# Turning q and k of three attentions by DMA transposes from SP, with expert weights issued from ScalarE

## The chip, the cores and the metric

The program runs on one core of one Trainium2 chip. The metric is the device time of one execution in microseconds (us), from launch to the last instruction on the slowest core; here there is only one core. Lower is better.

## The reference

Six layers are applied in turn to x (16 batch elements of 256 tokens x 256 channels, float32), with a layer norm of the residual sum after each:

```python
x = _layernorm(x + _L0_attn_ref(x, ...))                # a: 16 heads of 16, rotary, Taylor softmax
x = _layernorm(x + _L0_xattn_ref(x, ctx, ctx, mask))    # b: 16 heads, masked softmax, keys from ctx
x = _layernorm(x + _L0_ffn_ref(x, ...))                 # c: 8 experts, two chosen per token
x = _layernorm(x + _L1_attn_ref(x, ...))                # d: convolutions, delta rule, two FIR filters
x = _layernorm(x + _L1_xattn_ref(x, ctx, ctx))          # e: 16 heads, softmax, no projections
x = _layernorm(x + _L1_ffn_ref(x, ...))                 # f: FP4-rounded gate/up/down
```

In b and e:

```python
scores = jnp.einsum('bhqd,bhkd->bhqk', Q, K) / math.sqrt(D_K)
attn = jax.nn.softmax(scores, axis=-1)
context = jnp.einsum('bhqk,bhkd->bhqd', attn, V)
```

Layer a has (1 + s + s*s/2), divided by its sum, in place of the softmax. Layer d convolves each channel causally with 4 taps (q, k, v), and v again with 3 and with 31 taps.

## The kernel before

**Stages and lags.** Each batch element passes through the layers a, b, c, d, e, f. Iteration n of the program works on element n in a and b, n-1 in c, n-2 in d, n-3 in e and f (`LAG`, line 65), so 19 iterations are made and 13 of them hold all six layers. Within an iteration the order of the work is written out by hand: `BODY` (line 96) is one list of named segments, and every engine runs its own part of each segment in that order. Each engine executes in order, so an instruction that waits holds back everything that stands behind it on its engine.

**q and k of an attention.** q and k are split into bf16 parts that together keep float32 precision: for each token and head, six terms of 16 columns are laid side by side in `split` (96 columns, 102 with the columns for the mask and the row maximum). ScalarE makes casts and copies (`part_copies`, L1205), VectorE the differences (`split_rest`, L1550 and L1556); the last write of VectorE raises the signal p3, the last of ScalarE `copies`. A score product needs heads on partitions by their columns, so `split` must be turned: TensorE does this (`split_turn`, L731), 32 transposes for q and 32 for k in each attention, through the PSUM banks 0 to 3 (`turn_qk`). ScalarE (L1215) and VectorE (L1564) each copy two of the four banks of q and of k into `qT` and `kT`. In b and e the products `maxima` (L752) follow, whose row maxima VectorE takes (L1571); then three columns of `split` are filled with the shift and q is turned again (`turn_again`, segment `again`), and the final scores are made (L765).

**What stands around the turns in an iteration.** For e: `d_in c_in e_turnq e_turnk c_gate e_max0 d_proj e_max1`. For b: `b_turnq b_turnk d_scan2 b_max0 d_scan3`. For a: `a_turnq c_up2a c_up2b c_down2a f_round0 d_fir0 d_place c_down2b a_turnk c_up3a c_up3b c_down3a f_round1 d_fir1 c_down3b c_up4a c_up4b`, and the first score only later, after `f_down` and `d_one4`. The segments `f_round0` and `f_round1` are VectorE's FP4 rounding (from L1448 to L1457), whose result TensorE transposes (L1149).

**SP's queue.** SP issues all DMAs: inputs, the output, the small block DMAs of d (L544 to L559), and the expert weights (`layer_c`, L536 for c_w1, L538 for c_w2, 512 KB each). Two slots hold expert weights, so a load waits until TensorE has finished with the expert two before.

**VectorE's filters.** The taps of the convolution (L1749) and of the FIR filters (`fir`, L1788 and L1790) add into an accumulator. After each tap over all its channels comes `link`: the last instruction raises a semaphore and VectorE waits for it before the next tap.

```python
 def link(g, ins):
     chain[g] += 1
     ins.then_inc(s_chain[g], 1)
     dve.wait_ge(s_chain[g], chain[g])
```

Of the kernel before, what the change touches and what calls it, by code (L numbers as in the profile page):

```python
# [33 lines left out]
MASK0, MAX0, SLOT = QK, QK + 3, QK + 6  # L34
VS = 32
# [15 lines left out]
PT_SLOTS = 8  # L51
W_SLOTS = 2
CONSTANTS_MASK = 7
CONSTANTS = 54 - 4 * (LEVELS - 2) + 2
# [125 lines left out]
def bank_uses():  # L180
# [21 lines left out]
    turned("e", "turnq", "qT")  # L202
    turned("e", "turnk", "kT")
# [6 lines left out]
    for t in range(T):  # L210
        turned("a", "turn" + "qk"[t], "qk"[t] + "T")
        at(f"f_round{t}", (f"f_hT{t}a", 0), (f"f_hT{t}b", 1))
# [7 lines left out]
    turned("b", "turnq", "qT")  # L220
    turned("b", "turnk", "kT")
# [36 lines left out]
def decoder(nc, d, out):  # L258
    ctx = ExitStack()
    with ctx:  # L260
# [62 lines left out]
        yf, yc, yd = tok("yf"), tok("yc"), tok("yd")  # L323
# [51 lines left out]
        eye = sb("eye", [P // 2, BB, BB])[:, :, :]  # L375
# [12 lines left out]
        fshort, flong, qn, kn, kb, vb, vt, uu, dd = (sub(2, S) for _ in range(9))  # L388
        beta = sb("beta", [P, T, DH])
# [15 lines left out]
        f_sc = sb("f_sc", [P, 2, FF // BLK])  # L405
# [17 lines left out]
        for l in "abe":  # L423
            att[l] = {n: signal(f"{l}_{n}", 1) for n in
                      ("p1", "r1", "p2", "p3", "copies") + (("src",) if l != "e" else ("v",)) + (("shift",) if l != "a" else ())}
        c_diff = signal("c_diff", 1)
# [62 lines left out]
        def _(sp):  # L489
# [32 lines left out]

            def layer_a(b):
# [4 lines left out]
                sp.dma_start(ctxf[:, :, :], at(d["ctx"], b)).then_inc(*ctxf_in.up)  # L528

            def layer_c(b):  # L530
                for e in range(E):
                    yield "c_in" if e < W_SLOTS else f"c_up{e - 1}a"
                    slot = e % W_SLOTS
                    before = (e - W_SLOTS, b) if e >= W_SLOTS else (E + e - W_SLOTS, b - 1)
                    sp.wait_ge(*PS.filled(f"c_h{before[0]}_1", before[1]))
                    sp.dma_start(c_w1[:, slot], d["c_w1"][e].rearrange("(c p) n -> p c n", p=P)).then_inc(*c_w1in[slot].up)  # L536
                    sp.wait_ge(*PS.filled(f"c_y{before[0]}", before[1]))
                    sp.dma_start(c_w2[:, slot], d["c_w2"][e].rearrange("(c p) n -> p c n", p=P)).then_inc(*c_w2in[slot].up)  # L538
# [22 lines left out]
            def layer_e(b):  # L561
                yield "e_in"
                sp.wait_ge(*xo["x6_ready"](b, 0))
                sp.dma_start(ctxb[:, :, :], at(d["ctx"], b)).then_inc(*ctxb_in.up)

# [5 lines left out]
            batches(sp, {"a": layer_a, "c": layer_c, "d": layer_d, "e": layer_e, "f": layer_f})  # L571
# [4 lines left out]
        def _(pool):  # L576
# [38 lines left out]
            for l in range(BASE, LEVELS - 1):  # L615
# [10 lines left out]
            made(pool.memset(eye, 0.0))  # L626
            made(pool.affine_select(out=eye, in_=eye, compare_op=ALU.not_equal, fill=1.0, base=0,
                                    pattern=[[1, BB], [-1, BB]], channel_multiplier=0))
# [32 lines left out]
            def layer_d(b):  # L661
# [8 lines left out]
                step(pool.tensor_copy(blkT, eye))  # L670
# [23 lines left out]
        def _(pe):  # L694
# [1295 lines left out]
```

## Time and profile before

| | |
|---|---|
| median of 3 runs | 4020.27 us (4013.6 to 4021.18) |
| the profiled execution's own time | 4020.32 us |
| its span, first to last instruction | 4018.6 us |
| TensorE matmul / weight load busy | 83% / 63% |
| VectorE, ScalarE, GpSimd busy | 65%, 41%, 8% |
| mean granted TensorE clock | 0.932 of full |
| DMA engines busy, mean | 14.2% of 16 engines by the main queue, 171.27 MB |

The profile is one execution. A row of the timeline gives the start in us from the span's start, the duration in us, the engine, the line, the operation, output and input with their shapes, the count of merged instructions, and in brackets the idle time before it with what ended that. PE is TensorE's matmuls (transposes among them), PEld its weight loads, DVE VectorE, ACT ScalarE, POOL GpSimd, SPq SyncE's DMA issues. The granted clock (PEclk) is 1.00 at 2.4 GHz and 0.50 at 1.2 GHz.

### The profile page before, as it was taken

Reading aid. Unit: us, or ns where it says so; the run is one execution under the profiler, and the core shown is the slowest. Engines: PE = TensorE matmul, PEld = TensorE weight load, DVE = VectorE, ACT = ScalarE, POOL = GpSimd, SP = SyncE. Lnnn points to the kernel's source line nnn. Section 1 sums busy time; section 2 is a strip of 40 time slices with the busy share of each in tenths; the row PEclk is TensorE's granted clock in tenths of the full one; section 3 lists DMA queues with packets and bytes.
Section 4 is the critical chain, followed back from the end, with each engine's and each line's share of the span. In section 5 each row is a group of like instructions: output and inputs, shape, how many; then the busy total and the mean of one; then the engine's idle time right before and its main releaser. Section 6 shows DMA issues by size and latency. Waiting matters only on the chain.

```text
span 4018.6 us, 58753 instructions
## 1 busy us (share of the span) xinstructions
PE 3319.1 (83%) x22532; PEld 2516.8 (63%) x22532; DVE 2621.5 (65%) x5927; ACT 1637.0 (41%) x3066; POOL 341.3 (8%) x696
## 2 busy tenths in 40 slices
PE   1678988889898988889898888989898888978664
PEld 0356766767676676767576676767576676756442
DVE  4324667685776767676676768577676768666653
ACT  1433453444435354443435354443535344442311
POOL 1000101010100101010100101010010101010100
PEclk9788999999999999999999999999999999999776
DMA  2011202111111112111111111111111211111000
GB/s 71 22 58 48 64 28 63 35 56 43 40 49 42 55 35 59 40 51 43 38 56 38 54 35 57 42 46 48 43 48 35 64 35 56 43 34 49 9 6 3
DMA packets 185713, 175.03 MB, mean 44 GB/s; under 512 B 59208, under 2 KB 147936, under 8 KB 185440
## 3 DMA queue, kind: packets, MB, share of 16 engines
q1 hardware_dynamic: 185440, 171.27, 14.2%
q8 instruction: 186, 3.05, 0.3%
q14 instruction: 87, 0.71, 0.1%
HBM read 156.55 MB, written 14.68 MB: 43 GB/s over the span
## 4 chain that ended last, share of the span: by engine, by line
PE 51%; DVE 28%; ACT 10%; issue 6%; POOL 3%; DMA 1%; PEld 0%; SPq 0%; PEldq 0%; DVEq 0%; POOLq 0%; ACTq 0%
PE bank L697 18%; PE bank L932 6%; ACT pt_f L1194 5%; DVE nm_f L1571 5%; PE bank L731 5%; PE bank L785 4%; DVE region L1790 4%; PE bank L765 3%; ACT qT_f L1215 2%; PE bank L1014 2%; PE bank L778 1%; PE bank L752 1%; PE bank L1093 1%; PE bank L1025 1%; POOL rn L666 1%
## 5 line engine op out<-in xcount | busy, mean ns | idle before, releaser
L1194 ACT ACTIVATE pt_f<-bank 128x512 f32<-128x512 f32 x768 | 416.2, 594 | 281.8 <-PE bank L765 280.1
L932 PE MATMUL bank<-c_w,c_hb 128*128 128x256 f32 x2048 | 509.4, 388 | 9.8 <-PEq L1167 6.4
L697 PE MATMUL bank<-xTc,c_w 128*128 128x256 f32 x2048 | 485.6, 386 | 15.6 <-DVE yc L1723 14.5
L1790 DVE SCALAR_TENSOR_TENSOR region<-vpad,cols,region 128x256 f32<-128x256 f32 x1024 | 450.5, 481 | 15.4
L932 PEld LDWEIGHTS bank<-c_w,c_hb 128*128 128x128 f32 x2048 | 377.4, 192 | 97.1 <-issue 25.8
L697 PEld LDWEIGHTS bank<-xTc,c_w 128*128 128x128 f32 x2048 | 381.4, 192 | 77.7 <-DVE yc L1723 20.2
L1293 ACT ACTIVATE c_hb<-bank,cols 128x256 f32<-128x256 f32 x512 | 215.0, 471 | 476.6 <-PE bank L697 476.6
L1571 DVE TENSOR_REDUCE nm_f<-bank 128x2 f32<-128x512 f32 x512 | 315.6, 683 | 127.6 <-PE bank L752 125.5
L731 PE MATMUL bank<-identb,split_f 128*102 128x128 bf16 (+1 forms) x4096 | 291.8, 239 | 113.8 <-DVE split_f L1556 72.7
L765 PE MATMUL bank<-qT_f,kT_f 102*128 102x256 bf16 (+1 forms) x1536 | 276.8, 282 | 115.7 <-ACT pt_f L1194 92.7
L731 PEld LDWEIGHTS bank<-identb,split_f 128*102 128x102 bf16 (+1 forms) x4096 | 279.3, 142 | 144.3 <-DVE split_f L1556 86.0
L765 PEld LDWEIGHTS bank<-qT_f,kT_f 102*128 102x128 bf16 (+1 forms) x1536 | 112.5, 98 | 278.7 <-ACT pt_f L1194 221.6
L1215 ACT COPY qT_f<-bank 102x1024 bf16<-102x1024 bf16 (+1 forms) x160 | 156.1, 1014 | 166.0 <-PE bank L731 166.0
L1194 ACT ACTIVATE xTf<-bank 128x512 f32<-128x512 f32 x112 | 66.8, 597 | 353.6 <-PE bank L706 324.8
L785 PE MATMUL bank<-pt_f,v_f 128*32 128x256 f32 x3072 | 205.8, 394 | 0.4 <-PEq L1167 0.3
L1723 DVE SCALAR_TENSOR_TENSOR yc<-bank,comb,yc 128x256 f32<-128x256 f32 x256 | 111.8, 478 | 134.6 <-PE bank L932 127.3
L643 POOL TENSOR_TENSOR rstd_f<-ve_f,neghalf 128x2 f32<-128x2 f32 x80 | 57.1, 714 | 1608.2 <-DVE ve_f L1533 1608.2
L1564 DVE COPY qT_f<-bank 102x1024 bf16<-102x1024 bf16 (+1 forms) x160 | 110.5, 691 | 117.2 <-PE bank L731 117.2
L1827 DVE TENSOR_TENSOR region<-region,bank 128x512 f32<-128x512 f32 x128 | 85.1, 685 | 119.1 <-PE bank L1025 110.0
L1205 ACT COPY split_f<-split_f 128x512 bf16<-128x512 bf16 x288 | 159.6, 618 | 3.0
L697 PE MATMUL bank<-f_wgu,xTf 128*128 128x352 f32 x512 | 157.9, 467 | 0.7 <-ACT xTf L1194 0.7
L752 PE MATMUL bank<-kT_f,qT_f 99*128 99x256 bf16 x1024 | 145.6, 280 | 10.3 <-DVE kT_f L1564 3.9
(310 smaller groups left out, 5470.8 us busy)
## 6 DMA issues: line engine op xcount, KB each, us to landing
c_w<-in_c_w SPq DMA_DIRECT2D x256, 512.0 KB, 3.9
gram_scratch<-region SPq DMA_DIRECT2D x32, 256.0 KB, 2.2
x<-in_x SPq DMA_DIRECT2D x16, 256.0 KB, 4.4
x<-in_ctx SPq DMA_DIRECT2D x16, 256.0 KB, 4.5
ctxb<-in_ctx SPq DMA_DIRECT2D x16, 256.0 KB, 4.3
out_dram<-x SPq DMA_DIRECT2D x16, 256.0 KB, 2.2
region<-gram_scratch SPq DMA_DIRECT2D x128, 8.0 KB
inverse_scratch<-region SPq DMA_DIRECT2D x32, 64.0 KB
```

What stands on the lines that cost most here:

```text
L697: mm = pe.matmul(out_ap, l, r, start=(i == 0), stop=(i == len(pairs) - 1))
L731: mm = pe.transpose(o[0:n, j, t * P:(t + 1) * P], a.split[:, t, which, 4 * i + j, 0:n], identb[:, :])
L752: mm = pe.matmul(PS[use][:, t * S:(t + 1) * S], a.qT[0:MAX0, h, t * P:(t + 1) * P], a.kT[0:MAX0, h, :], start=True, stop=True)
L765: mm = pe.matmul(PS[use][:, c * S:(c + 1) * S], a.kT[0:rows_, h, c * P:(c + 1) * P], a.qT[0:rows_, h, :], start=True, stop=True)
L785: mm = pe.matmul(o[32 * j:32 * j + 32, :], a.v[:, c, h, :], a.pt[:, h % PT_SLOTS, c, :], start=(c == 0 and not taylor), stop=(c == T - 1), ...
L932: mm = pe.matmul(PS[use][:, t * D:(t + 1) * D], c_hb[:, k, t * P:(t + 1) * P], c_w2[:, e % W_SLOTS, k, :], start=(k == 0), stop=(k == HC - 1))
L1194: act.activation(dst, PS[use].rearrange("p (c s) -> p c s", c=c), func, **kw).then_inc(*PS.drained(use))
L1205: ins = act.copy(slot(n), slot(0) if n else per_head(src[:, :, :]))
L1215: act.copy(dst[0:n, 4 * i:4 * i + 4, :], PS[f"{use}{i}"].bitcast(BF16).rearrange("p (h s) -> p h s", h=4)[0:n])\
L1293: ins = act.activation(c_hb[:, k, :], PS[use][:, i * S:(i + 1) * S], ACT.Relu, bias=col("b1")[:, e * HC + k:e * HC + k + 1])
L1571: dve.tensor_reduce(a.nm[:, :, h], PS[use].rearrange("p (t s) -> p t s", t=T), AX.X, ALU.max, negate=True)\
L1790: ins = dve.scalar_tensor_tensor(dst[:, c, :], x, w_[:, c, k:k + 1], dst[:, c, :], ALU.mult, ALU.add)
```

## The change

1. **Turning by DMA.** `split` is padded from 102 to 128 columns a head, and `qT`, `kT` to 128 partitions. `turn_qk` and its copies on ScalarE and VectorE are gone from a, b and e. SP waits for p3, `copies` and the last earlier score, and then issues eight DMA transposes for each attention, each of [128 tokens, 8 heads x 128 columns] in bf16 (256 KB): four for heads 0 to 7 (signal `turned0`), four for heads 8 to 15 (`turned1`). TensorE waits for `turned0` ahead of the first group of heads and for `turned1` ahead of the third. The second turn of q in b and e (`again`) stays on TensorE.
2. **Expert weights from ScalarE.** The loads c_w1 and c_w2 leave SP and are issued by ScalarE: experts 0 and 1 at the start of `c_in`, expert e+1 behind the activations of `c_up{e}a`.
3. **VectorE's waits.** The convolution, the FIR filters and the layer norm's statistics wait for the tap (or half) that they add to, no longer for all of the tap before (`mark` in the place of `link`).
4. **Room.** `yd` shares memory with `fshort`, `f_sc` lies in `pt`; the block identity `eye` is no longer kept: GpSimd makes it in place each time (a memset and a select instead of a copy).

```diff
-                s.split = sb(f"split_{g}", [P, T, 2, H, SLOT], BF16)
-                s.qT = sb(f"qT_{g}", [SLOT, H, S], BF16)
-                s.kT = sb(f"kT_{g}", [SLOT, H, S], BF16)
+                s.split = sb(f"split_{g}", [P, T, 2, H, PITCH], BF16)
+                s.qT = sb(f"qT_{g}", [P, H, S], BF16)
+                s.kT = sb(f"kT_{g}", [P, H, S], BF16)
...
+            def turn_heads(b, l, last, half):
+
+                if half == 0:
+                    sp.wait_ge(*att[l]["p3"](b))
+                    sp.wait_ge(*att[l]["copies"](b))
+                    sp.wait_ge(*PS.filled(*last))
+                n = H // HALVES
+                for i, dst in enumerate((at_.qT, at_.kT)):
+                    for t in range(T):
+                        sp.dma_start_transpose(dst[:, half * n:(half + 1) * n, t * P:(t + 1) * P],
+                                               at_.split[:, t, i, half * n:(half + 1) * n, :].rearrange("p h d -> p (h d)")
+                                               ).then_inc(*att[l][f"turned{half}"].up)
+
+            def turns(b, l, last):
+                yield f"{l}_turnq"
+                turn_heads(b, l, last, 0)
+                yield f"{l}_turnk"
+                turn_heads(b, l, last, 1)
...
-            def turn_qk(b, l, a, n):
-                yield f"{l}_turnq"
-                pe.wait_ge(*att[l]["p3"](b))
-                pe.wait_ge(*att[l]["copies"](b))
-                for i in range(4):
-                    split_turn(b, l, a, n, f"{l}_qT", 0, i)
-                yield f"{l}_turnk"
-                for i in range(4):
-                    split_turn(b, l, a, n, f"{l}_kT", 1, i)
-
             def maxima(b, l, a, g):
-                if g == 0:
-                    for i in range(4):
-                        pe.wait_ge(*PS.taken(f"{l}_kT{i}", b))
+                if g % 2 == 0:
+                    pe.wait_ge(*att[l][f"turned{g // 2}"](b))
...
+            def load_expert(b, e):
+
+                slot = e % W_SLOTS
+                before = (e - W_SLOTS, b) if e >= W_SLOTS else (E + e - W_SLOTS, b - 1)
+                act.wait_ge(*PS.filled(f"c_h{before[0]}_1", before[1]))
+                act.dma_start(c_w1[:, slot], d["c_w1"][e].rearrange("(c p) n -> p c n", p=P)).then_inc(*c_w1in[slot].up)
+                act.wait_ge(*PS.filled(f"c_y{before[0]}", before[1]))
+                act.dma_start(c_w2[:, slot], d["c_w2"][e].rearrange("(c p) n -> p c n", p=P)).then_inc(*c_w2in[slot].up)
+
             def layer_c(b):
                 yield "c_in"
+                for e in range(W_SLOTS):
+                    load_expert(b, e)
                 evac(b, "c_xT", xTc[:, :, :])
...
                         ins.then_inc(*PS.drained(use))
+                        if m == 0 and W_SLOTS <= e + 1 < E:
+                            load_expert(b, e + 1)
...
+            def mark(g, ins):
+
+                chain[g] += 1
+                ins.then_inc(s_chain[g], 1)
+                return chain[g]
...
                         if k == 0:
                             ins = dve.tensor_scalar(dst[:, c, :], x, w_[:, c, 0:1], None, ALU.mult)
                         else:
+                            dve.wait_ge(s_chain["d"], summed[c])
                             ins = dve.scalar_tensor_tensor(dst[:, c, :], x, w_[:, c, k:k + 1], dst[:, c, :], ALU.mult, ALU.add)
-                    return ins
+                        if (K, k, c) == (KL, KL - 1, C - 1):
+                            ins.then_inc(*d_fir.up)
+                        else:
+                            summed[c] = mark("d", ins)
```

**How it moves instructions: SP.** On SP before, from the inputs of a to just behind the blocks of d (in_c_w is an expert's weights, gram_scratch and inverse_scratch hold the blocks of d):

```order
L526 DMA x<-in_x 128x2x256
L528 DMA x<-in_ctx 128x2x256
L544 DMA gram_scratch<-region 128x512 x2
L549 DMA region<-gram_scratch 8x16x16 x8
L536 DMA c_w<-in_c_w 128x2x512
L538 DMA c_w<-in_c_w 128x4x256
L553 DMA inverse_scratch<-region 8x8x256 x2
L559 DMA region<-inverse_scratch 16x16x16 x8
L536 DMA c_w<-in_c_w 128x2x512
L538 DMA c_w<-in_c_w 128x4x256
```

The same stretch now:

```order
L544 DMA x<-in_x 128x2x256
L546 DMA x<-in_ctx 128x2x256
L556 DMA gram_scratch<-region 128x512 x2
L561 DMA region<-gram_scratch 8x16x16 x8
L531 DMA_TRANSPOSE qT_f<-split_f 128x8x128 x2
L531 DMA_TRANSPOSE kT_f<-split_f 128x8x128 x2
L565 DMA inverse_scratch<-region 8x8x256 x2
L571 DMA region<-inverse_scratch 16x16x16 x8
L531 DMA_TRANSPOSE qT_f<-split_f 128x8x128 x2
L531 DMA_TRANSPOSE kT_f<-split_f 128x8x128 x2
```

The sixteen weight loads of an iteration left the queue and 24 transposes came in; the first four of a stand ahead of the block DMAs of `d_place`.

**TensorE, around the turns of b.** Before, from the last `c_up6a` to the first maxima (L731 turns, L1060 to L1073 are `d_scan2`, L752 maxima):

```order
L697 MATMUL bank<-xTc,c_w 128x256 x4
L731 MATMUL bank<-identb,split_f 102x128 x64
L1060 MATMUL bank<-region 128x64 x2
L1062 MATMUL bank<-Sb,wTn 128x64 x2
L1060 MATMUL bank<-region 128x64 x2
L1062 MATMUL bank<-Sb,wTn 128x64 x2
L1073 MATMUL bank<-region 128x64 x4
L752 MATMUL bank<-kT_f,qT_f 128x256 x8
```

Now:

```order
L709 MATMUL bank<-xTc,c_w 128x256 x4
L1058 MATMUL bank<-region 128x64 x2
L1060 MATMUL bank<-Sb,wTn 128x64 x2
L1058 MATMUL bank<-region 128x64 x2
L1060 MATMUL bank<-Sb,wTn 128x64 x2
L1071 MATMUL bank<-region 128x64 x4
L753 MATMUL bank<-kT_f,qT_f 128x256 x8
```

The 64 transposes are gone; only `d_scan2` stands between p3 and the maxima, which now wait for `turned0`.

**ScalarE, at the start of c.** Now, from the last split copies of e to the gate (xTd and xTc are the transposed inputs of d and c):

```order
L1202 COPY split_f<-split_f 128x2x16x16 x2
L1191 ACTIVATE xTd<-bank 128x512
L1271 DMA c_w<-in_c_w 128x2x512
L1273 DMA c_w<-in_c_w 128x4x256
L1271 DMA c_w<-in_c_w 128x2x512
L1273 DMA c_w<-in_c_w 128x4x256
L1191 ACTIVATE xTc<-bank 128x512
L1282 ACTIVATE gw<-gw 128x2
```

The four loads of experts 0 and 1 stand between xTd and xTc, just behind p3 of e; before they stood on SP, and the turn copies of e stood here behind xTc.

## Rows read from the trace of the kernel before

**Rows 1.** The page, parts 1 and 4: busy time by engine, and the chain.

```profile
PE 3319.1 (83%) x22532; PEld 2516.8 (63%) x22532; DVE 2621.5 (65%) x5927; ACT 1637.0 (41%) x3066; POOL 341.3 (8%) x696
...
PE 51%; DVE 28%; ACT 10%; issue 6%; POOL 3%; DMA 1%; PEld 0%; SPq 0%; PEldq 0%; DVEq 0%; POOLq 0%; ACTq 0%
```

**Rows 2.** Timeline around the turns of e, iteration 7; d_w is d_proj.

```profile
1477.10 1.29 DVE L1556 TENSOR_TENSOR split_f<-rest_f,split_f 128x512 bf16<-128x512 f32 x2 [1.21 <-ACT split_f L1205]
1478.45 5.96 PE L731 MATMUL bank<-identb,split_f 128*102 128x128 bf16 x64 [3.12 <-DVE split_f L1556]
1478.63 0.59 ACT L1194 ACTIVATE xTc<-bank 128x512 f32<-128x512 f32 x1
...
1484.24 1.01 PE L697 MATMUL bank<-c_wg,xTc 128*128 128x8 f32 x8
...
1485.39 1.03 PE L752 MATMUL bank<-kT_f,qT_f 99*128 99x256 bf16 x8
```

**Rows 3.** Windows of 1 us there: busy us by engine, PEclk, DMA share, GB/s.

```profile
1476.00:1477.00 1.00, 0.00 (x0) 0.00 (x0) 0.00 (x0) 1.00 (x2) 0.00 (x0) 0.62 0.00 0
...
1483.00:1484.00 1.00, 1.00 (x20) 1.00 (x19) 0.45 (x1) 1.00 (x2) 0.00 (x0) 0.96 0.00 0
```

**Rows 4.** Timeline around the turns of b, same iteration.

```profile
1645.97 1.29 DVE L1556 TENSOR_TENSOR split_f<-rest_f,split_f 128x512 bf16<-128x512 f32 x2 [1.82 <-ACT split_f L1205]
...
1647.47 4.01 PE L731 MATMUL bank<-identb,split_f 128*102 128x128 bf16 x64
...
1651.31 0.61 PE L1060 MATMUL bank<-region 128*128 128x64 f32 x4
...
1654.54 1.04 PE L752 MATMUL bank<-kT_f,qT_f 99*128 99x256 bf16 x8
```

**Rows 5.** Windows elsewhere in that iteration: an idle TensorE, and the clock.

```profile
1533.00:1534.00 1.00, 0.00 (x0) 0.00 (x0) 1.00 (x1) 0.21 (x1) 0.29 (x1) 1.00 0.40 147
1534.00:1535.00 1.00, 0.00 (x0) 0.00 (x0) 1.00 (x4) 0.00 (x0) 0.00 (x0) 0.64 0.92 342
```

**Rows 6.** Timeline around the turns of a: L1448 starts a rounding, L1149 uses it.

```profile
1556.49 1.99 PE L731 MATMUL bank<-identb,split_f 128*96 128x128 bf16 x32
...
1559.12 0.87 DVE L1448 TENSOR_REDUCE f_sc<-pt_f 128x44 f32<-128x704 f32 x1
...
1565.78 0.87 PE L1149 MATMUL bank<-ident,pt_f 128*128 128x128 f32 x6 [1.73 <-DVE pt_f L1457]
...
1577.33 4.54 DVE L1790 SCALAR_TENSOR_TENSOR region<-vpad,cols,region 128x256 f32<-128x256 f32 x10
1577.47 0.88 PE L1149 MATMUL bank<-ident,pt_f 128*128 128x128 f32 x6 [1.73 <-DVE pt_f L1457]
...
1582.84 1.99 PE L697 MATMUL bank<-xTc,c_w 128*128 128x256 f32 x8 [1.04 <-DVE yc L1723]
```

**Rows 7.** VectorE's convolution in the timeline, six independent taps between waits.

```profile
1504.96 7.41 DVE L1749 SCALAR_TENSOR_TENSOR region<-region,cols 128x256 f32<-128x256 f32 x18
```

**Rows 8.** The page, part 6: DMA issues, KB each, median us to landing.

```profile
c_w<-in_c_w SPq DMA_DIRECT2D x256, 512.0 KB, 3.9
gram_scratch<-region SPq DMA_DIRECT2D x32, 256.0 KB, 2.2
```

**Rows 9.** Windows with DMA at work: pieces of 64 bytes, then weights.

```profile
1563.00:1564.00 1.00, 1.00 (x4) 0.59 (x4) 0.97 (x2) 0.00 (x0) 0.00 (x0) 1.00 0.35 33
...
1567.00:1568.00 1.00, 1.00 (x6) 0.87 (x5) 0.96 (x3) 0.26 (x2) 0.00 (x0) 1.00 0.87 332
```

**Rows 10.** Timeline of SP's issues: a weight load, the blocks, and one iteration later.

```profile
1500.54 0.37 SPq L536 DMA_DIRECT2D c_w<-in_c_w  x1
...
1561.37 3.77 SPq L559 DMA_DIRECT2D region<-inverse_scratch  x8
...
1645.77 0.51 SPq L564 DMA_DIRECT2D ctxb<-in_ctx  x1
...
1729.24 0.37 SPq L536 DMA_DIRECT2D c_w<-in_c_w  x1
```

More of the change, by code:

```diff
@@ L528, in layer_a, with layer_b @@
                 sp.dma_start(ctxf[:, :, :], at(d["ctx"], b)).then_inc(*ctxf_in.up)
[L530 to L538, printed above, removed]
+                yield from turns(b, "a", ("e_s15", b - LAG["e"]))
+            def layer_b(b):
+                yield from turns(b, "b", ("a_s15", b))
             def layer_d(b):
@@ L564, in layer_e @@
                 sp.dma_start(ctxb[:, :, :], at(d["ctx"], b)).then_inc(*ctxb_in.up)
+                yield from turns(b, "e", ("b_s15", b + LAG["e"] - 1))
             def layer_f(b):
@@ L669, in layer_d @@
                 step = lambda ins: link(ins)
-                step(pool.tensor_copy(blkT, eye))
+                step(pool.memset(blkT, 0.0))
+                step(pool.affine_select(out=blkT, in_=blkT, compare_op=ALU.not_equal, fill=1.0, base=0,
+                                        pattern=[[1, BB], [-1, BB]], channel_multiplier=0))
                 pool.wait_ge(*d_blocks_in(b))
@@ L854, in layer_a @@
                 to_tokens(b, "a_v", xTf, a_wv)
-                yield from turn_qk(b, "a", a, QK)
                 for g in range(4):
                     yield f"a_score{g}"
-                    if g == 0:
-                        for i in range(4):
-                            pe.wait_ge(*PS.taken(f"a_kT{i}", b))
+                    if g % 2 == 0:
+                        pe.wait_ge(*att["a"][f"turned{g // 2}"](b))
                     yield from heads(b, "a", a, g, QK, True)
@@ L883, in layer_b @@
                 to_tokens(b, "b_q", xTf, b_w[:, 0])
-                yield from turn_qk(b, "b", a, SLOT)
                 for g in range(4):
@@ L1113, in layer_e @@
             def layer_e(b):
-                yield from turn_qk(b, "e", a, SLOT)
                 for g in range(4):
@@ L1241, in layer_a @@
                 part_copies(b, "a", a, qs, ks, 2)
-                yield "a_turnq"
-                turned(b, a, "a_qT", a.qT, QK)
-                yield "a_turnk"
-                turned(b, a, "a_kT", a.kT, QK)
                 for g in range(4):
@@ L1526, in ln_stats @@
             def ln_stats(b, l, g, src):
+                made = [mark(g, dve.bn_stats(stats[g][:, t, :], src[:, t, :])) for t in range(T)]
                 for t in range(T):
-                    ins = dve.bn_stats(stats[g][:, t, :], src[:, t, :])
-                link(g, ins)
-                for t in range(T):
+                    dve.wait_ge(s_chain[g], made[t])
                     ins = dve.bn_aggr(mv[g][:, t, :], stats[g][:, t, :])
@@ L1748, in layer_d @@
                             dve.wait_ge(*PS.taken(f"d_{'qkv'[j // 2]}", b))
+                        if k:
+                            dve.wait_ge(s_chain["d"], tapped[j])
                         ins = dve.scalar_tensor_tensor(cv[:, j, :], pre[:, j, k:k + S], w[:, j, k:k + 1], cv[:, j, :], ALU.mult, ALU.add)
-                    link("d", ins) if k < 2 else ins.then_inc(*d_cv.up)
+                        if k < 2:
+                            tapped[j] = mark("d", ins)
+                ins.then_inc(*d_cv.up)
                 yield "d_silu"
@@ L1796, in filters @@
                     for k in range(i * len(taps) // n, (i + 1) * len(taps) // n):
-                        ins = fir(*taps[k])
-                        if k == len(taps) - 1:
-                            ins.then_inc(*d_fir.up)
-                        else:
-                            link("d", ins)
+                        fir(*taps[k])
                 yield "d_fir0"
```

44 lines of the change are left out of this document (11 added, 33 removed).

## The prediction

> **What bounds the kernel now.** I read the page's busy times and chain first: TensorE is busy 83% and carries 51% of the chain, VectorE 28%, ScalarE 10% [rows 1]. No engine bounds alone; the bound changes from place to place, so a saving counts where its engine is waited for. The issue rows of the trace give the length of a full iteration: the same weight load comes at 1500.54 and 1729.24 [rows 10], so 228.7 us, and what is worked out for one iteration counts 16 times (each attention is run 16 times; the partial iterations at both ends are taken as alike). Then I read the timeline at the three places where q and k are turned, and the windows for the clock.
>
> - At e [rows 2] everything waits in a line: p3 ends at 1478.39, TensorE has stood for 3.12 us, makes 64 transposes in 5.96 us and starts the maxima at 1485.39, **7.0 us after p3**. The windows say why 64 transposes take 5.96 here and 4.01 at b [rows 2, 4]: the granted clock is at 0.62 in the slice from 1476 and 0.96 in the slice from 1483 [rows 3]; between them TensorE ran at 1.2 GHz.
> - At b [rows 4] p3 ends at 1647.26, the transposes take 4.01 us, `d_scan2` from 1651.31 on, and the maxima start at 1654.54, **7.3 us after p3**, 3.2 of which are `d_scan2`.
> - At a [rows 6] the first score comes over 30 us after p3, so a transfer is hidden there. VectorE's rounding is the bound: TensorE waits 1.73 us for each of the two.
>
> **The change, part by part.**
>
> *The wait for a transfer, L.* L is the time from p3 until four DMA transposes (1 MB) have landed. No transpose by DMA is in this trace, so a transfer of 256 KB is bounded from both sides. Plain pieces of 1 to 2 KB: the window with weights moves 332 GB/s at a share of 0.87 [rows 9], 382 at a full share, so 0.68 us. Pieces of 64 bytes: 33 GB/s at 0.35 [rows 9], 94 at a full share, so 2.8 us (at the 33 really moved, 8 us). A turned transfer is likely cut into more pieces than a plain one but into none below 64 bytes; I take 1.1 us, nearer to the plain end because a head's row is 256 bytes. The latency comes on top: 256 KB leave SBUF in 2.2 us [rows 8], 1.5 without the transfer. Alone, L = 1.5 + 4 x 1.1 = 5.9 us; the ends are 4.2 and 12.7.
> The page "DMA: Bandwidth & Descriptors", section "Latency and other measured facts", of the Trainium skill gives DMA transposes 261 GB/s. By that, 1.0 us for each and L = 5.5, an estimate; no run here shows it so far.
>
> *Weights in the way.* ScalarE now issues the four loads of experts 0 and 1 between the copies of xTd and xTc, just behind p3 of e, at 1478.7 in the old times; at 0.37 us an issue [rows 10] all four are out 1.5 us later. They are 2 MB, 5.4 us of the DMA engines at 382 GB/s, beside the first transposes. At b the two loads of expert 7 come 1.2 us after p3: 2.7 us. Before, they were issued earlier, beside nothing urgent. If the two queues share the engines evenly, half of that lies in front: L is 5.9 + 2.7 = **8.6 at e** and 5.9 + 1.3 = **7.2 at b**. The bounds are none and all.
>
> *e.* TensorE loses 64 transposes but cannot start the maxima before p3 + 8.6: 8.6 - 7.0 = +1.6 us. And the low clock, which the transposes used to bear, now falls on other work. It rose 4.6 us after steady work began (1478.45 to about 1483.0 [rows 2, 3]); those 4.6 us now begin with the maxima and `d_proj`, which do half as much in them: +2.3. Together **+3.9 us**. ScalarE's 1.5 us of issues in front of xTc only delay the gate, which ends in the wait.
>
> *b.* TensorE reaches the maxima at p3 + 3.3 and waits till 7.2: 7.2 - 7.3 = -0.1. It stands 3.9 us. After 2.5 us of standing the clock fell in the slice from 1534 [rows 5], so it falls here too: +2.3, none if the wait is short. **+2.2 us**. With the 4 us of transposes gone, what is late next is the transfer.
>
> *a.* Both transpose sets of 1.99 us go, and VectorE's four copies in front of the two roundings. The first rounding starts at the end of the yc addition, about 1557.4, in place of 1559.12 [rows 6], 1.7 us sooner; the second gains another 1.1 us from the copies and 0.3 from the filters between. So the second L1149 comes 3.1 us earlier, less than the 4.0 that TensorE gives up, because it waits for VectorE. Then ten FIR taps and the yc addition stand before the matmul at 1582.84: another 0.5. **-3.6 us**.
>
> *The links.* Ten FIR taps take 4.54 us, 0.454 each; the convolution, with a link every six, 0.412 [rows 6, 7]. Without waiting for the pair before, 0.1 us goes with each of 34 pairs: 3.4 us of VectorE an iteration. Where TensorE leads that is hidden; beyond the 0.8 counted at a I put **-0.5**.
>
> *ScalarE.* It loses 12 turn copies of 1 us an iteration and takes 16 issues of 0.37 us, always behind the activation that is waited for. At nothing; with that cover gone, at most 0.8 us at each of six places.
>
> *SP and the rest.* The blocks of `d_place` stood at 1561.37 [rows 10]; four transposes of a now precede them, 4.4 us, and TensorE asks for them 20 us later, so nothing. The context for e, issued at 1645.77, waits for eight transposes of b until about 1656 and is read at 1697: nothing. The weights for `c_up3a` are no longer behind the block DMAs. GpSimd's two instructions for one stand in its wait for the blocks. PSUM banks come free earlier. All at nothing.
>
> *Sum.* 3.9 + 2.2 - 3.6 - 0.5 = +2.0 us an iteration, times 16 = +32 us on the profiled execution's own 4020.32 (0.05 us above the median): **4052 us**, 0.8% slower. The sign turns on L: with the clock's price at both places the sum is zero where the two L have a mean of 6.9 us; the forecast has 7.9.
>
> **The rivals.**
>
> 1. *The transfer is short, and the kernel faster.* Place: the same two waits. If a transpose moves like a plain transfer, 0.68 us, and the queues hardly disturb each other, L is 4.2. At e, the gate (held by ScalarE's issues) holds the maxima until about p3 + 4.6: -2.4 +2.3. At b p3 + 4.2: -3.1, and the 0.9 us of standing leaves the clock alone. With -4.1: -7.3 an iteration, -117 us, 3903 us. For it: the engines are busy only 14% on average. Against it: the loads behind p3, and that small pieces moved far slower than weights [rows 9]. It decides from L below 6.9.
> The page "Advanced Engine Details and Errata", section "X-Bar Transpose (TRN2)", of the Trainium skill says that transposing DMAs are as fast as plain ones on this chip; that is this rival, and no row here shows it yet. I give it 0.3.
> 2. *The transfer is long.* At 2.8 us a transpose L is 12.7 at both: e +5.7 +2.3, b +5.4 +2.3, with -4.1: +11.6, +186 us, 4206 us. For it: many small pieces, and a queue whose issuing may itself take the time. Against it: at 94 GB/s the pieces of 64 bytes were bound by their issue. 0.2.
> 3. *ScalarE's queue is late with the weights.* Expert 4's first load would be issued near 1570 and read near 1576.6; landing takes 3.9 [rows 8], a slack of 2.6 us that transposes of a might eat. If each of six loads came 1 us late: +6 - 4.1 + 6.1, about +8, +128 us, 4148. 0.05.
> 4. That the change does not do what it says would be a second wait in place of the transposes at a too; its scores come 30 us later, so I give it no chance of its own.
>
> **How the numbers follow.** Forecast 0.45, rival 1 0.3, rival 2 0.2, rival 3 0.05. The forecast's own range, from L between 6.2 and 9.5 without or with the clock at b, is 3990 to 4100. The whole range takes in the values of rivals 1 and 2: 3900 to 4210. Faster by over 0.2% (8 us, about what a measurement of this kernel can tell from no change): 0.3 and 0.07 of the forecast, 0.37. Within 0.2%: 0.08. Slower: 0.55.
>
> **What would show it.** In the changed profile: the gap from p3 to the maxima at e (8.6 here, 7.0 before) and at b (7.2, 7.3 before); a TensorE that waits for DMA there; the granted clock still at 0.5 in `d_proj` and falling after p3 of b; `c_up4b` 3.6 us closer to p3 of a; filter taps of 0.41 us. An L under 6 at both places, or a clock that stays up, would make the forecast wrong, and so would a VectorE or ScalarE relief that shortens stretches between these three places, which I have put at 0.5 us.

## The result, and the profile after

The kernel as changed takes 4166.69 us (median of 4 runs, 4159.63 to 4177.01) where the one before, on the same chip, takes 4016.93: a ratio of **1.0368** (95% interval 1.0348 to 1.0388), 150 us or 9.4 us an iteration slower. 4052 was forecast: the sign was right, the loss almost five times too small. The profiled execution took 4171.6 us, its span 4169.9, the mean granted clock 0.878 (0.932 before).

The page, parts 1, 4 and 6, of the changed kernel, for [rows 1] and [rows 8]:

```profile
PE 3207.2 (77%) x19460; PEld 2399.0 (58%) x19460; DVE 2447.8 (59%) x5735; ACT 1451.0 (35%) x2874; POOL 348.3 (8%) x710
...
PE 47%; DVE 24%; ACT 10%; SPq 7%; issue 6%; DMA 3%; POOL 2%; PEldq 0%; DVEq 0%; POOLq 0%; ACTq 0%; PEld 0%
...
c_w<-in_c_w ACTq DMA_DIRECT2D x256, 512.0 KB, 4.8
...
qT_f<-split_f SPq DMA_TRANSPOSE x192, 4.3
kT_f<-split_f SPq DMA_TRANSPOSE x192, 3.4
```

TensorE is busy for 112 us less than before, VectorE for 174, ScalarE for 186 (GpSimd for 7 more), and the kernel is slower: work was taken off the engines and a wait put in its place. The chain has 7% of SP's queue and 3% of DMA, which had 0 and 1. The view of waits, of TensorE (engine, line, whose end it waited for, us in total, times, longest), names it:

```profile
PE bank L753 <- DMA kT_f<-split_f: 281.3, 35, 16.7
```

**Around e** (timeline, for [rows 2]; `d_w` is d_proj):

```profile
1521.63 1.29 DVE L1559 TENSOR_TENSOR split_f<-rest_f,split_f 128x512 bf16<-128x512 f32 x2 [1.20 <-ACT split_f L1202]
...
1521.65 0.37 ACTq L1271 DMA_DIRECT2D c_w<-in_c_w  x1
...
1522.96 5.74 SPq L531 DMA_TRANSPOSE qT_f<-split_f  x2
1528.74 4.01 SPq L531 DMA_TRANSPOSE kT_f<-split_f  x2
1532.80 2.71 SPq L531 DMA_TRANSPOSE qT_f<-split_f  x2
...
1534.86 1.89 PE L753 MATMUL bank<-kT_f,qT_f 99*128 99x256 bf16 x8 [8.67 <-DMA kT_f<-split_f]
1536.55 7.64 PE L709 MATMUL bank<-xTd,d_w 128*128 128x256 f32 x24
```

p3 ends at 1522.92. The two pairs of transposes of heads 0 to 7, with weights beside them, hold SP's queue for 5.74 and 4.01 us; the pair after them, nearly alone, for 2.71. The maxima start at 1534.86, **11.9 us after p3**, where it was 7.0. The windows there (columns as in [rows 3]):

```profile
1516.00:1519.00 3.00, 0.66 (x4) 0.42 (x4) 2.66 (x10) 1.61 (x4) 0.88 (x2) 1.00 0.00 0
...
1523.00:1526.00 3.00, 1.68 (x8) 1.69 (x8) 0.00 (x0) 0.86 (x2) 0.00 (x0) 0.50 0.96 318
...
1537.00:1541.00 4.00, 4.00 (x11) 3.19 (x10) 1.02 (x3) 0.80 (x2) 0.00 (x0) 0.50 1.17 150
1541.00:1545.00 4.00, 4.00 (x25) 3.55 (x24) 0.00 (x0) 2.64 (x7) 0.00 (x0) 0.98 0.33 111
```

TensorE idled and its clock went from 1.00 to 0.50; it is still at 0.50 (1.2 GHz) while d_proj runs without a gap from 1537 to 1541, and is back just behind. Before, with the clock up, the same products of `d_proj` took 5.35 us in place of 7.64, and the maxima 1.03 [rows 2] in place of 1.89:

```profile
1486.26 5.35 PE L697 MATMUL bank<-xTd,d_w 128*128 128x256 f32 x24
```

**Around b** (timeline, for [rows 4]), and two windows:

```profile
1693.28 1.29 DVE L1559 TENSOR_TENSOR split_f<-rest_f,split_f 128x512 bf16<-128x512 f32 x2 [1.82 <-ACT split_f L1202]
...
1694.60 2.81 SPq L531 DMA_TRANSPOSE qT_f<-split_f  x2
...
1694.99 0.42 ACTq L1271 DMA_DIRECT2D c_w<-in_c_w  x1
...
1697.45 6.66 SPq L531 DMA_TRANSPOSE kT_f<-split_f  x2
...
1706.10 1.89 PE L753 MATMUL bank<-kT_f,qT_f 99*128 99x256 bf16 x8 [7.97 <-DMA kT_f<-split_f]
```

```profile
1693.00:1696.00 3.00, 3.00 (x21) 2.56 (x20) 2.08 (x4) 2.38 (x6) 0.00 (x0) 1.00 0.07 13
...
1710.00:1715.00 5.00, 5.00 (x22) 4.07 (x23) 2.91 (x5) 1.68 (x4) 0.00 (x0) 0.50 0.37 89
```

p3 ends at 1694.57, so the maxima come **11.5 us after p3** (7.3 before). Here the first pair is through before the weights arrive and the second takes 6.66 us. The clock falls here too, where it stayed up before.

**All sixteen turns.** The two places above are one iteration. Counted from the timeline for every element (end of p3 to the first maxima), the median is **12.4 us at e** (7.0 before) and **10.3 us at b** (7.3 before): at e the place shown is on the low side, at b it is the longest of the sixteen. The last two turns of e, where the expert weights are no longer loaded, come 7.5 us after p3 in this same trace.

**Around a** (timeline, for [rows 6]), and the convolution and a piece of the FIR filters (for [rows 7]):

```profile
1608.68 1.28 DVE L1559 TENSOR_TENSOR split_f<-rest_f,split_f 128x512 bf16<-128x512 f32 x2
...
1632.27 1.99 PE L709 MATMUL bank<-xTc,c_w 128*128 128x256 f32 x8 [0.41 <-DVE yc L1718]
```

```profile
1559.04 7.16 DVE L1747 SCALAR_TENSOR_TENSOR region<-region,cols 128x256 f32<-128x256 f32 x18
...
1627.39 4.04 DVE L1794 SCALAR_TENSOR_TENSOR region<-vpad,cols,region 128x256 f32<-128x256 f32 x10
```

From p3 of a (1609.96; before, 1556.43) to `c_up4b` it is 22.3 us, where it was 26.4: 4.1 us gained, 3.6 forecast. A tap takes 0.40 us.

### The profile page after: what moved, and what is told of

Its sections match the earlier page's. It is cut to its first block, busy times and chain, and to the rows that moved or that the text cites. A ratio compares the mean times of both kernels' runs of the same rounds, so it can differ in the third digit from the quotient of the medians.

```text
span 4169.9 us, 52451 instructions
## 1 busy us (share of the span) xinstructions
PE 3207.2 (77%) x19460; PEld 2399.0 (58%) x19460; DVE 2447.8 (59%) x5735; ACT 1451.0 (35%) x2874; POOL 348.3 (8%) x710
## 4 chain that ended last, share of the span: by engine, by line
PE 47%; DVE 24%; ACT 10%; SPq 7%; issue 6%; DMA 3%; POOL 2%; PEldq 0%; DVEq 0%; POOLq 0%; ACTq 0%; PEld 0%
PE bank L709 16%; SPq L531 6%; ACT pt_f L1191 5%; PE bank L930 4%; PE bank L786 4%; PE bank L753 3%; PE bank L766 3%; DMA kT_f<-split_f 3%; ACT split_f L1202 2%; DVE nm_f L1574 2%; PE bank L1091 2%; DVE region L1794 2%; PE bank L1012 1%; PE bank L1023 1%; PE bank L779 1%
## 5 line engine op out<-in xcount | busy, mean ns | idle before, releaser
L709 PE MATMUL bank<-xTc,c_w 128*128 128x256 f32 x2048 | 500.6, 395 | 7.5 <-DVE yc L1718 6.7
L709 PEld LDWEIGHTS bank<-xTc,c_w 128*128 128x128 f32 x2048 | 396.5, 199 | 76.5 <-DVE yc L1718 12.7
L1794 DVE SCALAR_TENSOR_TENSOR region<-vpad,cols,region 128x256 f32<-128x256 f32 x1024 | 413.3, 477 | 0.0
L753 PE MATMUL bank<-kT_f,qT_f 99*128 99x256 bf16 x1024 | 190.3, 347 | 282.9 <-DMA kT_f<-split_f 281.3
L753 PEld LDWEIGHTS bank<-kT_f,qT_f 99*128 99x128 bf16 x1024 | 114.8, 120 | 338.8 <-DMA kT_f<-split_f 288.1
L709 PE MATMUL bank<-f_wgu,xTf 128*128 128x352 f32 x512 | 159.4, 471 | 12.6 <-DVE hf L1624 11.9
L1594 DVE RECIPROCAL rc_f<-bank 128x16 f32<-128x16 f32 x96 | 23.9, 249 | 204.9 <-PE bank L811 204.9
L709 PEld LDWEIGHTS bank<-f_wgu,xTf 128*128 128x128 f32 x512 | 98.3, 195 | 68.1 <-issue 17.6
L786 PEld LDWEIGHTS bank<-pt_f,v_f 128*32 128x32 f32 x3072 | 86.1, 111 | 84.5 <-issue 48.5
```

The lines of the kernel that those rows point to most:

```text
L709: mm = pe.matmul(out_ap, l, r, start=(i == 0), stop=(i == len(pairs) - 1))
L753: mm = pe.matmul(PS[use][:, t * S:(t + 1) * S], a.qT[0:MAX0, h, t * P:(t + 1) * P], a.kT[0:MAX0, h, :], start=True, stop=True)
L786: mm = pe.matmul(o[32 * j:32 * j + 32, :], a.v[:, c, h, :], a.pt[:, h % PT_SLOTS, c, :], start=(c == 0 and not taylor), stop=(c == T - 1), ...
L1794: ins = dve.scalar_tensor_tensor(dst[:, c, :], x, w_[:, c, k:k + 1], dst[:, c, :], ALU.mult, ALU.add)
```

## The experiments

Theory 1, after this reading: the loss is made at the two waits, at e and b, by the transfer, by the weight loads beside it and by the clock behind it; the rest of the change gains a little. Theory 2: ScalarE's queue, or DMA traffic in general, slows other work. Ratios are to the kernel before on the same chip, with their 95% intervals.

### One part at a time

**m_actw**: the kernel before, with part 2 (weights from ScalarE) alone.

```diff
-            def layer_c(b):
-                for e in range(E):
-                    yield "c_in" if e < W_SLOTS else f"c_up{e - 1}a"
...
+                        if m == 0 and W_SLOTS <= e + 1 < E:
+                            load_expert(b, e + 1)
```

> The kernel before with part 2 alone: the expert weights are issued from ScalarE at the places of the change, all turns stay on TensorE. Theory 1: without DMA transposes beside them the loads disturb nothing and ScalarE's issues lie behind what is waited for: within 0.2% of before (4010 to 4028). Theory 2 (ScalarE's queue is a cause of its own: its issues delay activations or come late with weights): 1 us or more at each of several experts, 4050 or more, and TensorE waiting for c_w in the waits.

Measured 4019.38 us, ratio 0.9991 (0.9982 to 1.0000). ScalarE's queue and the places of the loads cost nothing by themselves. Theory 2 has lost one half.

**m_marks**: the kernel before, with part 3 (VectorE's waits) alone.

```diff
+                            dve.wait_ge(s_chain["d"], summed[c])
                             ins = dve.scalar_tensor_tensor(dst[:, c, :], x, w_[:, c, k:k + 1], dst[:, c, :], ALU.mult, ALU.add)
...
-                            link("d", ins)
```

> The kernel before with part 3 of the change alone (VectorE waits for the tap it adds to, not for all of the tap before; the same in the layer norm's statistics). Theory 1 (the loss is made at the two waits for transfers, at e and b, and the other parts are small gains): FIR taps at 0.41 us in place of 0.454, 3 us of VectorE less in an iteration, of which 0.5 to 1.2 us count: 4000 to 4010 us, 0.2 to 0.5% faster than before. Rival (VectorE's taps are hidden everywhere, or the semaphores cost as much): within 0.1% of before.

Measured 4028.53 us, ratio 1.0018 (1.0006 to 1.0029): no gain. The expectation missed. VectorE's own work did become shorter (the FIR taps, before and here), and one of its waits for TensorE longer (before and here):

```profile
L1790 DVE SCALAR_TENSOR_TENSOR region<-vpad,cols,region 128x256 f32<-128x256 f32 x1024 | 450.5, 481 | 15.4
L1804 DVE SCALAR_TENSOR_TENSOR region<-vpad,cols,region 128x256 f32<-128x256 f32 x1024 | 413.2, 479 | 0.0
...
DVE yc L1723 <- PE bank L932: 127.3, 23, 16.3
DVE yc L1728 <- PE bank L932: 164.8, 37, 16.3
```

The 37 us that the taps save are waited away one step later, for TensorE. TensorE itself is busy for 19 us more than before [rows 1], at a mean granted clock of 0.921 for 0.932:

```profile
PE 3338.5 (83%) x22532; PEld 2533.1 (63%) x22532; DVE 2578.0 (64%) x5927; ACT 1635.2 (41%) x3066; POOL 339.3 (8%) x696
```

So its products were slower; why the clock is lower here is not known.

**m_aonly**: the change with e and b turned on TensorE as before; a alone is turned by DMA.

```diff
+PE_TURNS = "eb"
...
+                if l in PE_TURNS:
+                    if g == 0:
+                        for i in range(4):
+                            pe.wait_ge(*PS.taken(f"{l}_kT{i}", b))
```

> The changed kernel with the turns of e and b given back to TensorE; only those of a go through the DMA transposes. Theory 1: the 4.1 us that the changed kernel gains at a stay, and both losses go: 4.1 and 0.5 to 1 us of VectorE's waits, 16 times: 3935 to 3950 us, about 2% faster than before. Theory 2 (transposes or ScalarE's loads slow other work wherever they run): not faster than before, 4020 or more.

Measured **3949.86 us**, ratio **0.9831** (0.9810 to 0.9852), faster than both kernels; theory 2, which expected 4020 or more, has lost its other half. So what the change does at a, with the weights from ScalarE and the marks, is worth 68 us by the ratio (66 were forecast: 16 x 4.1), and turning e and b by DMA loses all of it and 150 us more, 13.6 us an iteration.

**m_alink**: the same without the marks (the diff of m_marks taken back).

> Only parts 1 and 2 of the change and a alone of part 1: e and b are turned on TensorE, VectorE keeps its links of before. It differs from the kernel with a alone (3949.86, a ratio of 0.9831) in the links. The links alone cost nothing when they were taken away by themselves (1.0018). Theory (a's transposes carry the whole gain, the marks none): 3940 to 3955, within 0.3% of that kernel. Rival (the marks do pay once a's VectorE stretch is what the end waits for): 3965 to 3985.

Measured 3975.71 us, ratio 0.9895 (0.9876 to 0.9913). The rival was right: the same marks that were worth nothing alone are worth 0.65% (26 us) once a is turned by DMA. The pages of m_alink and of m_aonly:

```profile
PE 3260.2 (82%) x21508; PEld 2465.3 (62%) x21508; DVE 2581.5 (65%) x5863; ACT 1576.4 (40%) x3002; POOL 348.5 (9%) x710
...
PE 3249.8 (82%) x21508; PEld 2456.6 (62%) x21508; DVE 2534.4 (64%) x5863; ACT 1574.8 (40%) x3002; POOL 347.4 (9%) x710
```

With the marks VectorE still waits 30 us longer for TensorE at the yc addition (159.9 us in m_aonly, 130.1 in m_alink), as it did in m_marks, so that wait does not decide. What differs is TensorE's busy time in the profiled executions: 19 us more by the marks alone, 10 us less here, which is of the size of the difference between a loss of 7 us and a gain of 26. Why its products become slower in the one case and not in the other was not tested.

### The loads beside the transposes

**m_noload**: the change, with the expert weights loaded only once.

```diff
             def load_expert(b, e):
-
+                if b or e >= W_SLOTS:
+                    return
```

> The changed kernel with all expert loads left out but the first two, so every expert uses the first weights (that part of the result is not computed); nothing shares the DMA engines with the transposes. Theory 1 in the form that the loads stretch the transposes: a pair takes 2.7 us everywhere, the wait from p3 to the maxima falls from 11.9 and 11.5 to about 7.4 us at e and b, and the time by 4.3 us at two places, 16 times, to about 4030. Rival (a transpose queue has such stalls by itself): the pairs of 4 to 6.6 us stay, 4150 or more.

Measured 4029.39 us, ratio 1.0022 (1.0011 to 1.0033): 137 of the 150 us go with the loads (123 by the shorter waits, 16 times 4.9 and 2.8 us; most of the rest is clock, since `d_proj` takes 105.7 us in all for 115.0 in the change). Timeline around e, and two windows inside b's and e's waits:

```profile
1464.59 2.60 SPq L531 DMA_TRANSPOSE qT_f<-split_f  x2
1467.24 2.71 SPq L531 DMA_TRANSPOSE kT_f<-split_f  x2
...
1472.01 1.89 PE L753 MATMUL bank<-kT_f,qT_f 99*128 99x256 bf16 x8 [4.69 <-DMA kT_f<-split_f]
```

```profile
1404.00:1407.00 3.00, 0.00 (x0) 0.00 (x0) 0.00 (x0) 0.00 (x0) 0.00 (x0) 0.50 1.05 195
...
1470.00:1472.00 2.00, 0.00 (x0) 0.00 (x0) 0.40 (x3) 0.00 (x0) 0.00 (x0) 0.50 1.04 195
```

Alone, a transpose of 256 KB takes 1.35 us, and the maxima come 7.4 us after p3 at this e. Over all sixteen turns the median is 7.5 us at e and 7.5 at b. Single pairs still take longer without weights (3.40 us at the b whose window is shown, which makes its wait 8.4 us); what disturbs them is not known. The windows say why loads hurt it so: **the transposes alone bring the share of the sixteen DMA engines to 1.04 at 195 GB/s**, where weights moved 332 at a share of 0.87 [rows 9]. So there was hardly a free share for a load to use, and what it takes, the transposes wait for.

**m_late**: the change whole, with the loads of experts 0, 1 and 7 issued by ScalarE once the transposes have landed.

```diff
+                for e in range(W_SLOTS):
+                    if b + LAG["c"] >= LAG["e"]:
+                        act.wait_ge(*att["e"][("turned0", "turned1")[e]](b + LAG["c"] - LAG["e"]))
+                    load_expert(b, e)
...
                 yield "d_scan3"
+                if b + 1 < NB:
+                    if b + 2 < NB:
+                        act.wait_ge(*att["b"]["turned1"](b + 2))
+                    load_expert(b + 1, E - 1)
```

> The change whole, with the same expert loads from ScalarE issued behind the transposes: expert 0 once heads 0 to 7 of e have landed, expert 1 and expert 7 once all sixteen have. Nothing is left out. Theory (the loads beside the transposes stretch the wait, the low clock follows): both waits shrink as in the kernel without loads, p3 to the maxima 9 us at most at e and 8 us at b, and the time is 4010 to 4050, where the change had 4167. Rival (the loads are in the way wherever they stand, or come too late for c_up0a and c_up7a now): above 4100, with TensorE waiting for c_w.

Measured 4182.01 us, ratio 1.0421 (1.0398 to 1.0444): neither. TensorE's wait fell as theory 1 has it (medians of 7.5 us after p3 at e and at b), but ScalarE got two new ones in its place (views of waits, TensorE and ScalarE):

```profile
PE bank L753 <- DMA kT_f<-split_f: 179.7, 35, 16.8
```

```profile
ACT region L1309 <- DMA kT_f<-split_f: 190.6, 14, 15.6
...
ACT region L1368 <- DMA kT_f<-split_f: 130.9, 13, 11.0
```

L1309 is ScalarE's first copy of d_proj, L1368 its first of `d_scan3`. L1309 stands behind the wait for all sixteen heads, and expert 0's load, issued after eight, stretched the second half (a pair of 7.57 us). The experiment had the flaw that the edit made a wait on an in-order engine with other work behind it.

**m_tail**: the same loads issued by SP instead, behind the transposes in its own queue.

```diff
+            def layer_c(b):
+                for e, name in ((0, "c_gate"), (1, "c_comb"), (E - 1, "c_up6b")):
+                    yield name
```

> The change whole, nothing left out, with the loads of experts 0, 1 and 7 back on SP, behind the eight transposes of e and of b in its queue; experts 2 to 6 stay on ScalarE. No instruction of ScalarE waits for a transpose, and no load stands beside one at e or b. Theory (m_late lost at ScalarE's two new waits what it won at TensorE's): the waits of TensorE for kT add up to about 180 us as in m_late, no wait of ScalarE for it, and the time is that of the kernel without loads, 4015 to 4045. Rival (behind the transposes the loads come too late for c_up0a and c_up7a): above 4080 with TensorE waiting for c_w.

Measured 4032.07 us, ratio 1.0037 (1.0024 to 1.0050), as expected, with nothing left out: 135 us of the 150 come back by the place of three loads an iteration. TensorE's wait:

```profile
PE bank L763 <- DMA kT_f<-split_f: 174.7, 35, 16.9
```

The maxima come 7.5 us after p3 at e and at b (medians), as in the kernel without loads.

### The size of a transpose

**m_quart**: the change with four groups of four heads, sixteen transposes of 128 KB, of which TensorE awaits four ahead of each group.

```diff
-HALVES = 2
+HALVES = 4
...
-                if g % 2 == 0:
-                    pe.wait_ge(*att[l][f"turned{g // 2}"](b))
+                pe.wait_ge(*att[l][f"turned{g}"](b))
```

> The change with four groups of heads, the loads where the change has them. Theory: the first group is smaller, but the loads still stand beside it: 2.7 us or a little more less per wait, 4167 - 86 = about 4080 (4050 to 4110). If the stretch comes by the number of transposes beside the loads rather than by their bytes, it is less: above 4120.

Measured 4122.39 us, ratio 1.0267 (1.0246 to 1.0288). 44 us better than the change, half of what was expected, and just outside the range, where the rival begins (4120): at the e of the same iteration the first maxima come 9.95 us after p3 (11.9 in the change). The medians are 10.1 at e and 8.6 at b, for 12.4 and 10.3. A transpose of half the size does not take half the time: the last two turns of e, with no loads beside them, come 6.4 us after p3, for 7.5 in the change, so 1.1 us is the smaller transfer; the rest is likely the smaller number of bytes that share the engines with the loads, which no run tells apart from the number of transposes beside them. SP's queue, two transposes a row, and a window among them with no weights:

```profile
1461.50 2.58 SPq L531 DMA_TRANSPOSE kT_f<-split_f  x2
```

```profile
1464.00:1467.00 3.00, 3.00 (x13) 2.58 (x12) 1.33 (x3) 1.66 (x2) 0.00 (x0) 0.71 0.54 107
```

A transpose of 128 KB takes 1.29 us, nearly what one of 256 KB takes, and the DMA engines are only half busy (0.54, 107 GB/s). So something other than the moving of bytes is the limit here; what it is, no run shows.

**m_one**: one group of sixteen heads, four transposes of 512 KB.

```diff
-HALVES = 2
+HALVES = 1
...
-                if g % 2 == 0:
-                    pe.wait_ge(*att[l][f"turned{g // 2}"](b))
+                if g == 0:
+                    pe.wait_ge(*att[l]["turned0"](b))
```

> The change with one group of 16 heads: four transposes of 512 KB in each attention in place of eight of 256 KB, all awaited ahead of the first maxima. In four groups a transpose of 128 KB took 1.27 us of SP's queue, one of 256 KB 1.34. If that is a cost by the instruction (with a little by the byte), one of 512 KB takes 1.5 us, all sixteen heads have landed when eight had, and the time is 4130 to 4180. If above 256 KB it goes by the byte, 2.7 us each, the wait is 5 us longer at e and b: 4167 + 32 x 5 = 4330.

Measured 4319.15 us, ratio 1.0758 (1.0738 to 1.0779): the second case, nearly by the byte; the medians are 17.1 us at e and 14.5 at b, 4.7 and 4.3 longer. A second pair of b, with the loads' rest beside it at most (SP's queue in the timeline):

```profile
1515.41 4.76 SPq L530 DMA_TRANSPOSE kT_f<-split_f  x2
```

That is 2.4 us each, and 2.38 is also the median over k's transposes in this trace. So a transpose costs about 1.3 us at 128 and at 256 KB and 1.8 times that at 512 KB. Where between these sizes the bytes begin to count was not measured.

**m_qlate**: m_quart's and m_late's edits together.

> m_late with the heads turned in four groups in place of two, so that the first maxima wait for four transfers of 128 KB in place of 256 KB. Theory (a transpose's time goes by its bytes): each takes 0.68 us of SP's queue, the first group lands 2.7 us earlier at e and b, 2 x 2.7 x 16 = 86 us, and the idle time of TensorE falls to about 2 us, so that less of the clock is lost: 3900 to 3950, faster than the kernel before. Rival (a transpose has a fixed cost of a microsecond or so): the four small ones take as long as the four large, the time stays within 20 us of m_late or rises.

Measured 4413.39 us, ratio 1.0974 (1.0950 to 1.0998). Sixteen transposes last 21 us instead of 11, and ScalarE, as in m_late, waits for the last of them (270.5 and 266.4 us at its two places). The expectation missed, and its rival was right: a transpose of 128 KB takes as long as one of 256. It adds no cause.

### The clock

**m_fill**: the change, with products of no use ahead of TensorE's wait.

```diff
+                if g == 0:
+                    pe.wait_ge(*PS.free(f"{l}_m0", b))
+                    for i in range(16):
+                        pe.matmul(PS[f"{l}_m0"][:, 0:S], ident[:, :], ones[:, 0:S], start=True, stop=True)
```

> The change with 16 products of no use (128x128 by 128x256, float32, into a bank that the maxima overwrite) ahead of TensorE's wait for turned0 at e and at b. They take 6 to 7 us, inside the wait of 8 us, so they cost nothing themselves. Theory (3.1 and 3.4 us at each place are the low clock's): the granted clock stays near 1 in d_proj and d_scan3, minus 5 to 7 us an iteration, 4055 to 4090. Rival (the stretches behind the waits are slow for another reason, or the fill itself delays the maxima): within 20 us of 4167.

Measured 4087.24 us, ratio 1.0176 (1.0159 to 1.0193): **79 us faster than the change by adding work**. The groups by line for d_proj (busy us, mean ns), of the kernel before, of the change and of this kernel:

```profile
L697 PE MATMUL bank<-xTd,d_w 128*128 128x256 f32 x384 | 87.9, 386 | 0.0
...
L709 PE MATMUL bank<-xTd,d_w 128*128 128x256 f32 x384 | 115.0, 471 | 0.0
...
L709 PE MATMUL bank<-xTd,d_w 128*128 128x256 f32 x384 | 88.0, 387 | 0.0
```

The products take again what they took before the change. So the low clock after the waits cost at least 79 us, 2.5 us at each of 32 places; the mean granted clock is 0.921 here, 0.932 before, and at b the maxima come 0.3 us later than in the change (medians), so a little more may be due.

The same clock is why m_tail is no faster than the kernel before. It stands 82 us behind m_aonly, and the maxima come later than on TensorE by only 0.5 us at e and 0.3 at b, 13 us in all; the rest, 69 us, is about what m_fill gave back (an estimate: the two kernels also differ in who issues three loads). In m_tail d_proj's products still take 104.1 us, for 87.9.

**m_tailfill**: m_tail and 12 such products (`range(12)` in the edit above).

> m_tail with 12 products of no use (128x128 by 128x256, float32) ahead of TensorE's wait for turned0 at e and b, about 4.6 us each time. Theory: the idle 5 us of TensorE are filled, the clock stays up: m_tail less some 60 us, 3950 to 3990, faster than the kernel before. Rival (with the short wait the clock hardly falls, so there is nothing to win): within 15 us of m_tail.

Measured 4011.83 us, ratio 0.9989 (0.9978 to 1.0001): 20 us better than m_tail, a third of what was expected. The products at e and at b (each is recorded twice, so 24 for 12), and the maxima behind those of e:

```profile
1471.55 7.68 PE L760 MATMUL bank<-ones,ident 128*128 128x256 f32 x24
1479.07 1.04 PE L767 MATMUL bank<-kT_f,qT_f 99*128 99x256 bf16 x8
...
1640.32 5.40 PE L760 MATMUL bank<-ones,ident 128*128 128x256 f32 x24
```

At e they begin at the low clock, last 7.68 us instead of the 4.6 that I had put, and hold the maxima back to 10 us after the first transpose was issued (1468.97), where 7.4 would do. Over all sixteen turns the maxima come 9.8 us after p3 at e and 8.6 at b (medians), where m_tail has 7.5 at both: 3.4 us an iteration, 54 us, which is more than the 40 that are missing. A shorter fill was not tried.

## Why the prediction was right in sign and wrong in size

With the measured waits (medians of all turns) put into the forecast's own sum, 12.4 - 7.0 + 2.3 at e and 10.3 - 7.3 + 2.3 at b, less 4.1, is 8.9 us an iteration, 142 us; 150 were measured. (The one iteration shown, with 11.9 and 11.5, gives 154.) So the frame held and one term, L, failed, in both of its parts:

- **L alone: 5.9 forecast, 7.5 measured** at both places (m_noload, m_tail), 3.2 us an iteration too little. The failed step is "I take 1.1 us" for a transpose and "1.5 without the transfer" for the latency: in m_noload four transposes take 5.4 us of the queue in place of 4.4, and the maxima start 2.1 us after the last of them. I had left a rival in which a long transfer makes the kernel 186 us slower; its time was nearer the truth, but by a transpose of 2.8 us, which is not what happened.
- **Weights in the way: 2.7 forecast at e and 1.3 at b, measured 4.9 and 2.8** (12.4 - 7.5; 10.3 - 7.5), 3.7 us an iteration too little. The failed step is "if the two queues share the engines evenly, half of that lies in front". It had the order wrong, too: "just behind p3 of e" was 1.3 us ahead of it, since the two megabytes were issued from 1521.65 on, before the first transpose at 1522.96, and nearly all of their 5.4 us fell in front; at b, all of the 2.7. The bound "all" was the right value. m_noload and m_tail show this term, with the clock that goes with it: 137 and 135 us. With "all" and the old L alone the sum would have been 6.1 us an iteration, 4118 us; with the measured L alone and "half", 5.2 and 4103. It takes both.
- **The clock: 2.3 at each place forecast, 2.5 recovered by m_fill.** Right, and by the mechanism given, a little small (at the e shown, `d_proj` and the first maxima take 3.1 us longer); in m_tail it still falls.
- **a: -3.6 forecast, -4.1 measured; the taps -0.5.** With both, 66 us forecast, 68 measured by m_aonly. Without the marks the forecast has 2.8 us at a (its 3.6 less the 0.8 of the filters), 45 us, and m_alink measured 42 by its ratio. The taps are the other 1.3, 21 us; they brought 26 with a turned by DMA and none without, and that they hang on a the forecast did not say.
- **ScalarE's issues at nothing**: right (m_actw). The loads cost nothing from ScalarE in m_actw and 137 us in the change: it is not the queue, it is what stands beside them.
- **Rival 1**, a transfer as fast as a plain one, is out: transposes moved 195 GB/s at a share of 1.04, weights 332 at 0.87 [rows 9]. The rule cited beside it, of the Trainium skill's page "Advanced Engine Details and Errata", section "X-Bar Transpose (TRN2)", that transposing DMAs are as fast as plain ones, does not agree with these traces. The 261 GB/s of the Trainium skill's page "DMA: Bandwidth & Descriptors", section "Latency and other measured facts", was not reached at 256 KB (195), nor at 512 KB by the median (524288 bytes in 2.38 us, 220).
- **The range**: by its own condition (L of 6.2 at both places, no clock at b) the low end would be 3.7 us an iteration under before, 3961 us, not 3990. Nothing in the result hangs on it.

What the section "What would show it" named came in kind: TensorE waiting for DMA at both places, the clock at 0.50 in `d_proj` and behind p3 of b, `c_up4b` closer to p3 of a, taps of 0.40 us; the gaps of 12.4 and 10.3 in place of 8.6 and 7.2 are 110 of the 118 us by which the forecast missed the change's loss.

## What to carry to other kernels

Taking work off an engine gains nothing at a place where its successor then waits as long for the result from elsewhere: measure the new transfer from the signal that releases it to its use, with all traffic beside it, and use it only where that time is covered, as at a here. A DMA that is waited for should stand in front of bulk loads in one in-order queue; a load on another queue takes its engines, and a wait put in front of the load on a computing engine only moves the loss. And where TensorE has to wait some microseconds, count the slow products behind the wait, too.

## What the runs showed of the hardware that I had not expected

- A DMA transpose of bf16 takes 1.27 to 1.29 us of SP's queue for 128 KB, 1.35 for 256 KB and about 2.4 for 512 KB: at 128 KB the DMA engines are about half busy (0.54), at 256 KB their share is 1.04 at 195 GB/s, where weights moved 332 GB/s at 0.87.
- SP's queue is held longer when weights stand beside a transpose: a pair of 2.71 us lasted 6.66 at b in the change and 7.57 at e in m_late.
- Adding 16 useless products in a wait made the kernel 79 us faster, because d_proj's products went from 471 to 387 ns.
- A change on VectorE that was worth nothing alone (1.0018) was worth 0.65% beside another; TensorE was busy 19 us longer by it in the one case and 10 us less in the other.

The fastest kernel of the study is m_aonly, 3949.86 us, 1.7% under the kernel before.
